# A decoder layer with experts: gates on the experts' input rows, weights prepared one expert at a time, last score groups between expert chunks

## The reference

```python
x = x + attn(layernorm(x))                       # 16 heads of 64, causal, softmax over the query axis
x = x + xattn(layernorm(x), ctx, ctx)            # 16 heads of 8, softmax over the keys
# experts, on n = layernorm(x), E = 8, hidden 512
scores = n @ Wr + br                             # best two of eight
weights = softmax(where(indicator > 0, scores, -inf))
for i in range(E):
    xi = n * indicator[..., i:i+1]
    h = relu(xi @ W1[i] + b1[i])
    out += (h @ W2[i] + b2[i]) * weights[..., i:i+1]
x = x + out
```

## Time and profile before

| | us |
|---|---|
| median of 3 runs | 337.31 (335.52 to 338.12) |
| the profiled execution | 336.25 |
| its span, first to last instruction | 334.5 |

### The profile page before, as it was taken

How to read it: one execution, slowest core, us unless ns; L and a number is a source line. 1 busy time by engine, 2 the same in 40 slices (tenths; PEclk the granted TensorE clock), 3 DMA queues, 4 the chain that set the end, 5 groups by cost and what they waited for, 6 DMA issues and landing times.

```text
span 334.5 us, 5887 instructions
## 1 busy us (share of the span) xinstructions
PE 306.4 (92%) x2177; PEld 230.3 (69%) x2194; DVE 193.5 (58%) x450; ACT 163.4 (49%) x466; POOL 66.3 (20%) x102
## 2 busy tenths in 40 slices
PE   6789999999989898889687879899999999999995
PEld 2577677867866676556334333378999988998995
DVE  3677565457297875772877883363553564434432
ACT  1679767487646663663565778742212121212210
POOL 7991470301031003620300203020020000000000
PEclk9999999999999999999999997999999999999999
DMA  8800025511000100010016720000000001000001
GB/s 237 199 2 1 3 39 66 64 21 35 15 2 0 39 11 1 3 29 23 1 35 230 213 81 3 2 2 0 2 0 2 0 3 32 0 2 0 2 0 31
DMA packets 13884, 11.98 MB, mean 36 GB/s; under 512 B 2616, under 2 KB 10912, under 8 KB 13856
## 3 DMA queue, kind: packets, MB, share of 16 engines
q1 hardware_dynamic: 12272, 10.81, 13.6%
q10 hardware_dynamic: 1584, 0.80, 0.9%
HBM read 7.84 MB, written 0.52 MB: 25 GB/s over the span
## 4 chain that ended last, share of the span: by engine, by line
PE 76%; DVE 15%; issue 3%; ACT 3%; POOL 2%; DMA 1%; another core or an unknown queue 0%; DVEq 0%; ACTq 0%; POOLq 0%
PE ps L792 17%; PE ps L530 7%; PE ps L531 7%; PE ps L532 7%; PE ps L604 6%; PE ps L637 5%; PE ps L649 4%; DVE mneg L1128 4%; PE ps L682 4%; PE ps L718 4%; PE ps L703 3%; PE ps L611 2%; PE ps L639 2%; DVE negmax L1097 2%; DVE t_lo L1063 2%
## 5 line engine op out<-in xcount | busy, mean ns | idle before, releaser
L901 ACT ACTIVATE p<-ps,negmax 128x256 f32<-128x256 f32 (+1 forms) x128 | 52.6, 425 | 25.4 <-DVE negmax L1097 24.9
L792 PEld LDWEIGHTS ps<-w_raw,hid 128*128 128x128 f32 x512 | 59.5, 192 | 1.3
L792 PE MATMUL ps<-w_raw,hid 128*128 128x128 f32 x512 | 59.6, 275 | 0.0
L953 ACT ACTIVATE hid<-ps,b1T 128x512 f32<-128x512 f32 x32 | 21.9, 687 | 73.9 <-PE ps L532 73.9
L1128 DVE TENSOR_REDUCE mneg<-ps 128x2 f32<-128x512 f32 x64 | 42.1, 682 | 14.0 <-PE ps L682 13.3
L1097 DVE TENSOR_REDUCE negmax<-ps 128x2 f32<-128x512 f32 (+1 forms) x48 | 32.9, 686 | 19.6 <-PE ps L606 12.4
L930 ACT ACTIVATE px<-ps 128x512 f32<-128x512 f32 x64 | 35.3, 600 | 18.1 <-PE ps L703 15.1
L1220 DVE SCALAR_TENSOR_TENSOR resid<-ps,wgt,resid 128x128 f32<-128x128 f32 x64 | 18.0, 344 | 42.9 <-PE ps L792 42.9
L682 PE MATMUL ps<-k_st,q_mem 128*128 128x256 bf16 x128 | 24.7, 276 | 9.4 <-DVE mneg L1128 8.7
L1201 DVE TENSOR_SCALAR hid<-ps,b1T 128x512 f32<-128x512 f32 x32 | 23.8, 749 | 11.0 <-PE ps L532 10.9
L424 POOL TENSOR_SCALAR tmp<-mv 128x2 f32<-128x2 f32 x8 | 2.1, 268 | 141.2 <-DVE mv L1121 141.2
(11 more groups left out here) (171 smaller groups left out, 542.1 us busy)
## 6 DMA issues: line engine op xcount, KB each, us to landing
w_raw<-in_L_ffn_W SPq DMA_DIRECT2D x1, 2048.0 KB, 8.5
k_st<-k_part SPq DMA_DIRECT2D x12, 128.0 KB
q_mem<-q_part SPq DMA_DIRECT2D x48, 32.0 KB
w_in<-in_L_attn_W_qkv ACTq DMA_DIRECT2D x2, 384.0 KB, 6.3
w_in<-in_L_attn_W_qkv SPq DMA_DIRECT2D x2, 384.0 KB, 6.9
resid<-in_x SPq DMA_DIRECT2D x2, 256.0 KB, 4.1
p<-in_L_attn_W_o SPq DMA_DIRECT2D x1, 512.0 KB, 8.0
p<-in_ctx SPq DMA_DIRECT2D x1, 512.0 KB, 9.2
```

Source lines behind the costliest of these rows:

```text
L792: last = pe.matmul(ps[:, Y_BANK[k % 2], P * tt:P * tt + P], hid[:, k % 2, c, P * tt:P * tt + P], w2_sb[:, NC * e + c, :], start=(c == 0), ...
L901: last = act.activation(dst, bank[:, n * i:n * i + n], ACT.Exp, bias=negmax[:, kt, h:h + 1], accum_out=psums[:, kt, h:h + 1])
```

## The change

- The gate of a token (its weight for the expert) is put on the expert's input rows: as relu is homogeneous and a gate is never negative, gate x relu(n W1 + b1) = relu((gate x n) W1 + gate x b1). `gate_rows(k)` (unit X) picks the expert's row of the turned weights with one fp32r product and so spreads it over all partitions; VectorE multiplies (`gated`), ScalarE and VectorE make the high and low part (`gated_high`, `gated_low`).
- b1 is folded in: the last feature of the normed rows becomes 1, the last row of W1 becomes b1, and from the other rows W1's last row is subtracted (`first_weights`, on POOL; the row comes as a broadcast over 128 partitions, `last_rows`, 256 KB each). The router's weights are treated likewise; it now uses one fp32 tile `nT`.
- Y(k,c) sums over the experts in PSUM, three fp32r products of 512 columns for each chunk of 128 hidden features, with the relu in a high part (ScalarE, `relu_high`) and a low part (VectorE, `relu_low`). W2 gets high and low parts too (`second_high` on ScalarE, `second_weights` on POOL); `w1_lo` goes from VectorE to POOL (`first_low`). The accumulations on VectorE go; the sum of a half is copied (YE), turned (YO) and added at its end. b2 is one fp32 product in the same sum.
- W1 is loaded right after PJ(3), in front of stack_m(1) and stack_q(3).
- The router and gates of half 0 move to the slots of b = 2 and b = 3; the weights' preparation goes one expert at a time. CS(3,6), CS(3,7), CO(3,2), CO(3,3) and the last of batch 2's output stand between the chunks of expert 0, which therefore has two banks (2 and 5) for k < 2, and batch 3's scores have banks 0 and 1 only.

```diff
...
-            more = {(2, 1): [("b1", 0)], (3, 1): [("NT", 0)], (3, 7): [("RT", 0)]}
+            more = {(1, 6): [("WS", 0, 0)], (2, 1): [("WS", 0, 1)], (2, 6): [("WS", 0, 2)], (2, 7): [("NT", 0)],
+                    (3, 0): [("RT", 0)], (3, 2): [("GT", 0)], (3, 3): [("WT", 0), ("W2", 0, 0)], (3, 4): [("X", 0), ("WS", 0, 3)]}
...
                 if g == 0 and b >= 1:
                     slot += [("CO", b - 1, 3)]
                 slot += maxima_now[1:2] + (tail.get(g, []) if b else []) + maxima_now[2:] + more.get((b, g), []) + turn
-                if b == 2:
-                    slot += [("WS", 0, g)]
-                slots.append(slot)
-        slots.append([("CO", last, 3)])
-        extra = {0: [("GT", 0), ("oq0", last)], 1: [("WT", 0), ("oT0", last)], 2: [("B2", 0), ("oq1", last)], 3: [("oT1", last), ("wo", last)],
...
+                if (b, g) < (last, 6):
+                    slots.append(slot)
+
+        beside = {(0, 0): [("CS", last, 6, 0), ("CS", last, 6, 1), ("CO", last, 2)],
+                  (0, 1): [("CS", last, 7, 0), ("CS", last, 7, 1), ("oT0", last - 1)],
+                  (0, 2): [("oT1", last - 1)], (0, 3): [("CO", last, 3), ("wo", last - 1)],
+                  (1, 0): [("oq0", last)], (1, 1): [("oT0", last)], (1, 2): [("oq1", last)], (1, 3): [("oT1", last)],
+                  (2, 0): [("wo", last)], (4, 0): [("NT", 1)], (4, 2): [("RT", 1)], (5, 1): [("GT", 1)],
+                  (6, 1): [("WT", 1)], (9, 1): [("YO", 0, 0)], (9, 2): [("YO", 0, 1)]}
+        for k in range(2 * NE + 1):
+            slot = [("YE", 0, 0), ("YE", 0, 1)] if k == NE + 1 else []
+            slot += [("X", k + 1)] if k + 1 < 2 * NE else []
+            for c in range(NC):
...
+                if c == 1 and k + 1 < NE:
+                    slot += [("W2", 0, k + 1)]
+                if c == 3 and k + 4 < NE:
+                    slot += [("WS", 0, k + 4)]
+            if k % NE == 2:
+                slot += [("B2", k // NE)]
+            slots.append(slot)
+        slots.append([("YE", 1, 0), ("YE", 1, 1), ("YO", 1, 0), ("YO", 1, 1)])
...
+        G_BANK, Y_BANK = (0, 1, 2, 7), (4, 3)
+
+        def score_bank(b, k):
+
+            return k % 3 if b < B - 1 else k % 2
+
+        def out_bank(m):
+            return 3 + m % 2 if m < 2 * B - 1 else 3
+
+        def hidden_bank(k, c):
+            return (2, 5)[c % 2] if k < 2 else (0, 1, 2, 5)[c]
+
+        def last_in(bank, users):
+            return max((n for n, used in users if used == bank), default=-1)
+        score_banks = [score_bank(k // (2 * HP), k) for k in range(2 * HP * B)]
+        hidden_banks = [hidden_bank(n // NC, n % NC) for n in range(2 * NE * NC)]
...
             sp.wait_ge(s_misc, misc_at[("PJ", B - 1)] + 1)
             sp.dma_start(w1_raw[:, :].rearrange("p (e n) -> p e n", n=HID), w1.rearrange("e p n -> p e n")
-                         ).then_inc(s_w12[0], 16)
+                         ).then_inc(s_w1in, 16)
+            for i in range(LAST_RING):
+                last_rows(i)
+            stack_m(1)
+            sp.wait_ge(s_w1in, 16)
+            sp.dma_start(w1_raw[LAST:D, :], b1.rearrange("e n -> (e n)").unsqueeze(0)).then_inc(s_b1, 16)
+            stack_q(3)
+            sp.wait_ge(s_zero, 1)
+            for r in (0, LOW):
+                sp.dma_start(b2_sb[r:r + NE, :], b2).then_inc(s_b2, 16)
+            second_experts(0)
+            last_rows(3)
+            last_rows(4)
             stack_m(2)
-            sp.dma_start(w2_sb, w2.rearrange("e (c p) d -> p (e c) d", p=P)).then_inc(s_w12[1], 16)
+            last_rows(5)
+            second_experts(1)
+            last_rows(6)
+            last_rows(7)
             stack_m(3)
             for hf in range(2):
...
+                pool.tensor_tensor(w1_raw[0:LAST, cols], w1_raw[0:LAST, cols], w1_last[0:LAST, i % LAST_RING, :],
+                                   ALU.subtract).then_inc(s_wdiff, 1)
+
+            def first_low(i):
+                pool.wait_ge(s_whi, i + 1)
+                cols = slice(512 * i, 512 * i + 512)
+                pool.tensor_tensor(w1_lo[:, cols], w1_raw[:, cols], w1_hi[:, cols].bitcast(F32), ALU.subtract
+                                   ).then_inc(s_wlo, 1)
+
+            def second_weights(i):
+                pool.wait_ge(s_w2hi, i + 1)
+                cols = slice(512 * i, 512 * i + 512)
+                pool.tensor_tensor(w2_lo[:, cols], w2_raw[:, cols], w2_hi[:, cols].bitcast(F32), ALU.subtract
+                                   ).then_inc(s_w2lo, 1)
...
+            pool.memset(wgt_p[:, :, :].bitcast(F32), 0.0).then_inc(s_pick, 1)
+            pool.wait_ge(s_wr, 48)
+            pool.tensor_tensor(wr_sb[0:LAST, :], wr_sb[0:LAST, :], wr_last[0:LAST, :], ALU.subtract).then_inc(s_pick, 1)
+            for i in range(3):
+                first_weights(i)
             norm_3(0)
+            first_low(0)
+            first_weights(3)
+            first_weights(4)
             norm_3(1)
+            first_low(1)
+            for i in range(5, NE):
+                first_weights(i)
+            first_low(2)
+            second_weights(0)
             norm_3(2)
+            first_low(3)
+            second_weights(1)
+            second_weights(2)
             norm_3(3)
+            for i in range(4, NE):
+                first_low(i)
+                second_weights(i - 1)
+            second_weights(NE - 1)

...
                 elif kind == "RT":
+                    pe.wait_ge(s_pick, 3)
                     for t in ts:
-                        for i in range(2):
-                            last = pe.matmul(ps[:, 7, NE * (t % 4):NE * (t % 4) + NE],
-                                             n_parts[:, i, P * t:P * t + P].bitcast(F32), wr_sb[:, :],
-                                             start=(i == 0), stop=(i == 1))
+                        last = pe.matmul(ps[:, 7, NE * (t % 4):NE * (t % 4) + NE], nT[:, P * t:P * t + P], wr_sb[:, :],
+                                         start=True, stop=True)
...
+            def gate_rows(k):
+
+                e, hf = k % NE, k // NE
+                if k == 0:
+                    pe.wait_ge(s_mx_ev, 16 * B)
+                if e == 0:
+                    pe.wait_ge(s_misc_ev, misc_at[("WT", hf)] + 1)
+                ge(pe, s_xf, k)
+                pe.matmul(ps[:, X_BANK, :], pick[:, e, :], wgtT[:, 512 * hf:512 * hf + 512], start=True, stop=True
+                          ).then_inc(s_gt, 1)
+
...
             def hidden(k, c):

+                e, n = k % NE, NC * k + c
+                bank = hidden_banks[n]
+                if c == 0:
+                    if k < NE:
+                        pe.wait_ge(s_wlo, e + 1)
+                    pe.wait_ge(s_xlo, k + 1)
...
+                products(ps[:, bank, :], [w[:, e, P * c:P * c + P] for w in w1_p], [x[:, k % 2, :] for x in x_p]
+                         ).then_inc(s_h, 1)
...
+                bank = ps[:, Y_BANK[hf], :]
+                if c == 0:
+                    pe.wait_ge(s_w2lo, e + 1)
+                if e == 0 and c == 0:
+                    pe.wait_ge(s_pv_ev, last_in(Y_BANK[hf], ((m, out_bank(m)) for m in range(2 * B))) + 1)
+                pe.wait_ge(s_hd, NC * k + c + 1)
+                w, h = [w[:, NC * e + c, :] for w in w2_p], [x[:, c, :] for x in hid]
+                pe.matmul(bank, w[0], h[0], start=(e == 0 and c == 0), stop=False)
+                pe.matmul(bank, w[1], h[0], start=False, stop=False)
+                pe.matmul(bank, w[0], h[1], start=False, stop=(e == NE - 1 and c == NC - 1)).then_inc(s_y, 1)
+
...
+            def second_bias(hf):
+                pe.wait_ge(s_b2, 32)
+                pe.matmul(ps[:, Y_BANK[hf], :], b2_sb[:, :], wgtT[:, 512 * hf:512 * hf + 512].bitcast(F32),
+                          start=False, stop=False)
...
-            def relu(k, c):
+            def second_high(i):
+
+                act.wait_ge(s_w2in[i // (NE // 2)], 16)
...
+            def gated_high(k):
+                act.wait_ge(s_xf, k + 1)
+                ge(act, s_h, 4 * (k - 1))
+                act.copy(x_p[0][:, k % 2, :], x_f[:, k % 2, :]).then_inc(s_xhi, 1)
...
+            def relu_high(k, c):
                 act.wait_ge(s_h, 4 * k + c + 1)
-                ge(act, s_y, k - 1)
-                act.activation(hid[:, k % 2, c, :], ps[:, H_BANK[c], :], ACT.Relu,
-                               bias=b1T[:, NC * (k % NE) + c:NC * (k % NE) + c + 1]).then_inc(s_ha, 1)
-
-            def expert_copy(kind, hf):
+                ge(act, s_y, NC * (k - 1) + c + 1)
+                act.activation(hid[0][:, c, :], ps[:, hidden_banks[NC * k + c], :], ACT.Relu).then_inc(s_ha, 1)
...
-                dve.tensor_tensor(wgt[:, ts, :], hot[:, 0, ts, :], hot[:, 1, ts, :], ALU.add).then_inc(s_wgt, 1)
...
+                step(dve.tensor_tensor(wgt[:, ts, :], hot[:, 0, ts, :], hot[:, 1, ts, :], ALU.add))
+                dve.wait_ge(s_pick, 2)
+                step(dve.tensor_copy(wgt_p[:, ts, 0:NE], wgt[:, ts, :]))
```

(52 more changed lines are left out.)

285 lines of the change are left out of this document (151 added, 134 removed).

## The result

The changed kernel took 341.15 us (median of four runs, 340.28 to 342.53) against 337.0 us of the kernel before in the same comparison: ratio 1.013, 95% interval 1.0075 to 1.0185. The forecast was 331.5 us, range 326 to 339, and a chance of 0.11 for slower. It was wrong in sign and in range.

What follows compares the result with a forecast made beforehand. TensorE's own work was taken to bound the expert stage, a chain through TensorE, ScalarE and VectorE the stretch before. H(0,0) unmoved, stage 109.8 to 104.0 (-5.8), tail +0.5: -5.3, giving 331.5 us, range 326 to 339.

Steps and rivals of the forecast that it cites:

- The step that failed first: Expert stage: only `gated_low` could meet POOL, waiting up to 1.16 us within VectorE's slack, so no change in the sum.
- The gate chain: From wo(1)'s end near 199.7 us through norm, router, best_two, GT and WT to H(0,0) at 220.6, where it was before.
- rival B: Gate chain: ScalarE's two waits idle TensorE about 2 us each, lowering its clock; 2 x 1.7 if uncovered; chance 0.24.
- The stalls of the stage: First expert's slot, where `hidden` has two banks: 1.0 us added for stalls, making the stage 104.0.
- the bound of 5.6: Expert stage: upper case, a stall at each of eight uses of the two banks, 108.6 us against 103.0 without.
- The expert's pace: Steady part of the expert stage: 25 products of 0.233 us, 5.83 us an expert, against 6.38 before.
- 103.0 us of work in the stage: Expert stage on TensorE without stalls: 103.0 us after the change, against 109.8 before.
- the tail: After the last product: copies, turns, an addition and semaphores, 1.65 us against 1.13 before, priced at +0.5.
- the transfers: W1's load and three broadcasts ahead of stack_m(1): a cost of 0.5 us taken at CS(1,0,0).
- rival C: Slow broadcasts ahead of stack_m(1): CS(1,0,0) 9.5 us late, net +4.2, 341.5 us; chance 0.11.
- POOL in time: Expert stage: POOL's weight preparation is ready when needed; Y(1,0) has margin nothing, cost nothing, the other ones more.
- The norm with 127 columns: POOL's normalising passes: 0.93 us each instead of 0.45, two a batch, +1.0; the other bound was nothing.

Runs made afterwards that it cites:

- run 1: Changed kernel, with POOL's set-up block and first three W1 subtractions held until VectorE has split the queries of batch 3: 336.68 us, ratio 0.9977.
- run 3: Kernel before, with POOL's set-up block and three subtractions added on tiles that nobody else uses, no transfer moved: 339.8 us, ratio 1.0063.
- run 10: Changed kernel, with 22 idle products ahead of TensorE's two waits in the gate chain: 338.7 us, ratio 1.0014.
- run 7: Changed kernel with gate's Exp later, GT, WT, X(0) earlier, POOL's block behind the splits; then last batch's output steps and YO(0,1) later: 330.58 us.
- run 2: Kernel before, with W1's load and three 256 KB broadcasts put in front of stack_m(1), no extra POOL work: 337.07 us, ratio 0.9988.

## Why the prediction was wrong

**The step that failed first** is the sentence "by it only `gated_low`, one pass an expert, could meet POOL, a wait of up to 1.16 us in the slack of VectorE: the sum stays the same". POOL's new block begins at 164, not only its subtractions in the stage, and VectorE's `split_m(1)` and `split_q(3)` lie just there, with TensorE waiting for what follows them on VectorE. I had the row that shows the effect, read it as POOL held by VectorE, and looked for victims of the other direction in one stage only. The runs showed 4.5 us in its place (run 1; 2.8 in the kernel before, run 3). The hint of the cast at 163.69, 0.70 us beside POOL and 0.28 without, went unread. The reading of the rule was too narrow as well. The Trainium skill (SBUF — State Buffer, two separate sides) counts not only VectorE's operations with two SBUF inputs but also those in a two-port mode, and (VectorE: DVE Perf Modes, What auto-detection actually checks) a pass with one source, both source and destination in SBUF, qualifies for that mode if their outermost dimensions are even or equal. The trace agrees: the one-input casts went from 0.29 to 1.18 and 1.24 us, as the two-input pass from 0.43 to 1.37.

**The gate chain** was summed at 20.9 us from the end of wo(1) to H(0,0), and took 24.1. By its own terms: the norm was 0.8 quicker than priced (see below); best_two came at 2.9 us and not 1.9, by L1335's 1.20 us; the exponentials of (3,1) and CO(3,0) took 1.1 more, WT and CO(3,1) up to X(0) 1.5 more, both mostly by the clock (1.09 for 0.59, 1.94 and 1.82 for 1.07; run 10); the other 0.4 is spread over the small steps. This is rival B, even in its price: "twice that costs 2 x 1.7" against 2.9 measured. It had a chance of 0.24, and the prediction said what speaks for it (two idle stretches of 2 us each). To call that improbable was the second mistake: the exponentials that "cover much" stood behind the very Exp that waited, so they covered nothing: TensorE was busy 1.2 of the 4 us from 212 to 216.

**The stalls of the stage** were sized at 1.0 us and came at 4.0, inside the bound of 5.6. I had counted the two banks in the first expert's slot. The waits came in the second, from steps of the last batch put there only one place behind their producers (run 7: 2.0 us of them).

**What held.** The expert's pace (5.81 for 5.83); 103.0 us of work in the stage; the tail (1.7 for 1.65); no price for the transfers (run 2), so rival C's 341.5 us was met by the number and not by its mechanism; POOL in time, also for Y(1,0), where the margin was put at nothing (`second_weights(1)` ends at 243.4, X(3), which stands ahead of Y(1,0), starts at 245.39). The norm with 127 columns, priced at +1.0 by the row of the same width, cost nothing: the pass L543 takes 0.91 us for two of 127 columns, 0.455 each, against 0.449 for 128. The row of the other bound was the right one; the width is not what makes L439 slow.

**Sum** (of the two profiled executions, each of which has its own share of chance in the held steps and the clock). Forecast 331.0 for the profiled execution; +5.5 for the splits and the clock behind them, of which 0.7 comes back before wo(1), +3.2 for the gate chain, +3.0 for stalls, -0.3 in the tail: 341.7, as it took.
